# Attention softmax: the mask moves from GpSimd to VectorE, and two of eight heads are exponentiated by ScalarE straight out of PSUM

## The reference, cut to what matters

```
q, k, v = heads of layernorm(x) @ Wq + bq, ... @ Wk + bk, ... @ Wv + bv
scores  = einsum('bhqd,bhkd->bhqk', q, k) / sqrt(16)
scores  = where(adj[:, None] > 0, scores, -9e15)
attn    = softmax(scores, axis=-1)
x       = x + (einsum('bhqk,bhkd->bhqd', attn, v) as [b, n, 128]) @ Wo + bo
```

## Time and profile before

| | us |
|---|---|
| median of 3 runs | 1353.4 |
| the three runs | 1353.4, 1342.87, 1353.49 |
| the profiled execution, device time | 1348.24 |
| its span in the profile | 1346.4 |
| PE busy in the span | 1087.5 (81%) |
| DVE busy | 1032.0 (77%) |
| POOL busy | 922.8 (69%) |
| ACT busy | 837.6 (62%) |

### The profile page before, as it was taken

One profiled execution on the slowest core, in us unless ns is written; L12 is line 12 of the kernel. 1 busy time (PEld: TensorE's weight loads), 2 busy tenths in 40 slices (PEclk: granted clock), 3 DMA queues, 4 the chain that ended last, 5 costly groups with the idle time before them and its releaser, 6 DMA issues. The chain is left out here.

```text
span 1346.4 us, 39563 instructions
## 1 busy us (share of the span) xinstructions
PE 1087.5 (81%) x12580; PEld 783.5 (58%) x12581; DVE 1032.0 (77%) x2503; ACT 837.6 (62%) x1449; POOL 922.8 (69%) x929
## 2 busy tenths in 40 slices
PE   0788899889899988987288999799999999979200
PEld 0456666666666666665156677477777777768200
DVE  3578888888888888887467888487777777657498
ACT  0577777777777777774076788577766666567100
POOL 3336888888888888886766777457777777766300
PEclk9999999999999999999588999899999999999755
DMA  2113323333323333221334644244444444334399
GB/s 74 32 45 86 85 75 89 87 90 90 92 74 87 86 90 90 77 63 43 102 100 119 171 144 137 67 91 99 97 103 93 92 98 96 81 67 78 115 343 310
DMA packets 276548, 136.53 MB, mean 101 GB/s; under 512 B 195142, under 2 KB 254700, under 8 KB 276474
## 3 DMA queue, kind: packets, MB, share of 16 engines
q1 hardware_dynamic: 242938, 93.39, 28.7%
q0 software_dynamic: 16896, 33.86, 7.8%
q10 hardware_dynamic: 16640, 8.39, 2.1%
HBM read 47.95 MB, written 54.04 MB: 76 GB/s over the span
## 5 line engine op out<-in xcount | busy, mean ns | idle before, releaser
L1362 POOL DMA_INDIRECT pairs_dram<-x_rows x272 | 281.2, 1034 | 121.8 <-issue 81.8
L1040 ACT ACTIVATE hid<-Z,biases 128x512 f32<-128x512 f32 (+1 forms) x336 | 208.2, 632 | 141.1 <-PE Z L1008 88.7
L1055 DVE SCALAR_TENSOR_TENSOR h<-hid,h 128x512 f16<-128x512 f32 (+1 forms) x288 | 183.2, 649 | 54.3 <-ACT h L1031 49.6
L474 DVE TENSOR_REDUCE smax<-S 128x8 f32<-128x1024 f32 x128 | 155.8, 1217 | 73.7 <-PE S L730 72.2
L1020 PE MATMUL Y<-w,h 128*128 (+1 forms) x3168 | 192.8, 220 | 11.5 <-DVE h L1055 9.2
L1020 PEld LDWEIGHTS Y<-w,h 128*128 128x128 f16 x3168 | 185.6, 99 | 28.0 <-issue 10.6
L477 DVE TENSOR_TENSOR probs<-S,smax 128x1024 f32<-128x1024 f32 x128 | 156.8, 1225 | 14.4
L1153 POOL DMA_INDIRECT slots_dram<-x_rows,pair_slot x128 | 134.7, 1052 | 47.3 <-issue 27.3
L1008 PE MATMUL Z<-x_rows,w 128*128 128x512 f16 (+1 forms) x720 | 148.3, 352 | 11.3 <-DMA x_rows<-slots_dram 7.6
L619 ACT ACTIVATE probs<-probs 128x1024 f32<-128x1024 f32 x128 | 135.2, 1056 | 21.5 <-DVE probs L477 20.3
L339 POOL DMA_INDIRECT slots_dram<-x_rows,pair_slot x116 | 121.4, 1047 | 28.1 <-issue 16.8
(11 more groups left out here) (211 smaller groups left out, 2171.1 us busy)
## 6 DMA issues: line engine op xcount, KB each, us to landing
y_pairs<-pairs_dram SPq DMA_DIRECT2D x32, 512.0 KB, 5.9
x_res<-in_x_dram SPq DMA_DIRECT2D x32, 256.0 KB, 3.5
adj<-in_adj_dram SPq DMA_DIRECT2D x32, 256.0 KB, 3.2
xT_dram<-xT SPq DMA_DIRECT2D x32, 256.0 KB
xTu<-xT_dram SPq DMA_DIRECT2D x32, 256.0 KB, 2.9
out_dram<-x_res ACTq DMA_DIRECT2D x16, 512.0 KB, 7.9
pairs_dram<-x_rows POOLq DMA_INDIRECT x272
slots_dram<-x_rows,pair_slot POOLq DMA_INDIRECT x256
```

The costliest lines, as they stand in the source:

```text
L474: dve.tensor_reduce(smax[:].rearrange("p (r e) -> p r e", e=2), S_heads, AX_X, ALU.max).then_inc(s["max_done"], 1)
L1040: act.activation(self.hid[:, c, 0:w], self.bank(b, c)[:, 0:w], ACT.Gelu, bias=bias[:, c:c + 1], scale=1.0 / (XS * WS)).then_inc(self.gelu_ ...
L1055: dve.scalar_tensor_tensor(out=self.piece(b)[:, 1, c, 0:w], in0=self.hid[:, c, 0:w], scalar=HS, in1=self.piece(b)[:, 0, c, 0:w], op0=ALU.m ...
L1362: pool.indirect_dma_start(pairs_dram, bass.IndirectOffsetOnAxis(ap=pair_of[n][:, j:j + 1], axis=0), y_sb[n % NY][:, j], None, bounds_check ...
```

## The change

- qb, the scale of Q and the mask all change sign, so S holds minus the scores, and a masked place holds +9e15. The row maximum becomes a row minimum (smin, min_done in place of smax, max_done).
- SHIFTED = 6: VectorE subtracts for heads 0 to 5 only, as minimum minus S, with the operands swapped.
- Heads 6 and 7 (bank 3 of S) are read by ScalarE itself: one activation of 128 columns for each head, exp(-S + smin), with smin as a bias operand of one value for each partition. They stand ahead of the exponential of the other heads in ScalarE's order, and signal direct_done.
- The exponential in SBUF covers six heads.
- TensorE waits for direct_done as well as sub_done before it writes S again.
- mask moves from GpSimd to VectorE, to the end of slot 2 (mask(0) to the end of the step before group 0). GpSimd's wait for s_ps ahead of mask falls away.

```diff
+SHIFTED = 6
...
-        def mask(g, q):
-
-            pool.wait_ge(adj_loaded[q], (g // 2 + 1) * 16)
-            wait(pool, "s_ps", (g - 1) * GT)
-            pool.tensor_scalar(negmask[:, q], adj[:, q], 0.0, NEG, ALU.is_le, ALU.mult).then_inc(s["mask_ready"], 1)
...
-        mask(0, 0)
...
-            if has(g, -1):
-                mask(g + 1, (g + 1) % 2)
...
+        def mask(g, q):
+
+            dve.wait_ge(adj_loaded[q], (g // 2 + 1) * 16 if isinstance(g, int) else (g - q) * 8 + 16)
+            dve.tensor_scalar(negmask[:, q], adj[:, q], 0.0, -NEG, ALU.is_le, ALU.mult).then_inc(s["mask_ready"], 1)
...
-            dve.tensor_reduce(smax[:].rearrange("p (r e) -> p r e", e=2), S_heads, AX_X, ALU.max).then_inc(s["max_done"], 1)
-            wait(dve, "max_done", t + 1)
+            dve.tensor_reduce(smin[:].rearrange("p (r e) -> p r e", e=2), S_heads, AX_X, ALU.min).then_inc(s["min_done"], 1)
+            wait(dve, "min_done", t + 1)
             wait(dve, "pt_ps", 2 * (t - 1))
-            dve.tensor_tensor(probs[:, b].rearrange("p (r e) k -> p r e k", e=2), S_heads,
-                              smax[:].rearrange("p (r e) -> p r e", e=2).unsqueeze(3).to_broadcast([P, 4, 2, P]),
-                              ALU.subtract).then_inc(s["sub_done"], 1)
+            dve.tensor_tensor(probs[:, b, 0:SHIFTED].rearrange("p (r e) k -> p r e k", e=2),
+                              smin[:, 0:SHIFTED].rearrange("p (r e) -> p r e", e=2).unsqueeze(3).to_broadcast([P, SHIFTED // 2, 2, P]),
+                              S_heads[:, 0:SHIFTED // 2], ALU.subtract).then_inc(s["sub_done"], 1)
...
+                if j == 2 and has(g, -1):
+                    mask(g + 1, 1 - q)
...
-                act.activation(QT[:, q], M0[:, :], ACT.Identity, bias=qb[:], scale=0.25 / (XS * WS)).then_inc(s["q_sb"], 1)
+                act.activation(QT[:, q], M0[:, :], ACT.Identity, bias=qb[:], scale=-0.25 / (XS * WS)).then_inc(s["q_sb"], 1)
...
                 if has(t, 0, NT):
+                    wait(act, "min_done", t + 1)
+                    wait(act, "pt_ps", 2 * (t - 1))
+                    for h in range(SHIFTED, H):
+                        last = act.activation(probs[:, j % 2, h], S_heads[:, h // 2, h % 2], ACT.Exp,
+                                              bias=smin[:, h:h + 1], scale=-1.0)
+                    last.then_inc(s["direct_done"], 1)
                     wait(act, "sub_done", t + 1)
-                    pr = probs[:, j % 2]
+                    pr = probs[:, j % 2, 0:SHIFTED]
                     act.activation(pr, pr, ACT.Exp).then_inc(s["exp_done"], 1)
...
                     wait(pe, "sub_done", t)
+                    wait(pe, "direct_done", t)
```

More of the change, by code:

```diff
@@ L106, in attention_phase @@
     rs2s = sb("rs2s", [P, GT])
-    smax = sb("smax", [P, H])
+    smin = sb("smin", [P, H])
     turn = sb("turn_dve", [P, 1])
@@ L130, in attention_phase @@
              "top_done", "eq_done", "keyed", "key_done", "pick_done", "rest_done", "rank_ps", "counted", "slot_terms", "slot_ready",
-             "s_ps", "max_done", "sub_done", "exp_done", "pt_ps", "pt_sb", "pv_ps", "o_sb", "on_ps", "rec_done", "norm_done"]
+             "s_ps", "min_done", "sub_done", "direct_done", "exp_done", "pt_ps", "pt_sb", "pv_ps", "o_sb", "on_ps", "rec_done", "norm_done"]
     s = {n: sem(n) for n in names}
@@ L377, in _ @@
         dve.tensor_scalar(bv_mat, ones, cols[:, 2:3], None, ALU.mult).then_inc(prep, 1)
-        dve.tensor_scalar(qb[:], cols[:, 0:1], 0.25, None, ALU.mult).then_inc(prep, 1)
+        dve.tensor_scalar(qb[:], cols[:, 0:1], -0.25, None, ALU.mult).then_inc(prep, 1)
         dve.tensor_scalar(kb[:], parity[:], cols[:, 1:2], None, ALU.mult).then_inc(prep, 1)
@@ L521, in step @@
                 gather1(1, 1)
+                mask(0, 0)
                 return
@@ L673, in m0_task @@
                     wait(pe, "sub_done", NT)
+                    wait(pe, "direct_done", NT)
                 else:
```

## The result

The changed kernel takes 1387.6 us (median of 4 runs, 1386.1 to 1389.4) against 1348.1 us for the kernel before (median of 4, 1342.4 to 1353.5; the table of the time before has the median of three of them). The ratio is 1.0294, with a 95% interval from 1.0234 to 1.0353: about 39 us slower. The profiled execution has a span of 1384.8 us against 1346.4, +38.4. Of all the runs behind this text one, of the experiment "swapped", ran at a mean granted clock of 0.82 in place of about 0.94 and took 1451.9 us; it is in no median here.

What follows compares the result with a forecast made beforehand. The prediction took VectorE's chain, 18.18 us a group, as pace, replaced by a ring of 14.43 + 1.88 + 2.56 = 18.87; +0.69 over 31.75 groups is +21.9 us, 1348.2 to 1370 us. Range 1345 to 1395.

Steps and rivals of the forecast that it cites:

- a ring through ScalarE: Attention: S, PT0, pT0, PT1, pT1, direct pair, next S; 18.87 us a group against 18.18, +21.9 us; chance 0.50.
- S to pT1, four slots: Attention: from the start of the scores to the start of the second copy pT1, 14.43 us for a group.
- pT1 to the pair: ScalarE: from the start of pT1 to the start of the next activation, 0.47 us, four times 1.88 us.
- start of the pair to next S: Two direct activations of 355 ns, overlapping, 0.59 us, plus 0.05 until PE starts: 0.64, four times 2.56 us.
- 0.40 for K in slot 3: Slot 3: K's evacuation on ACT comes 0.81 us after S instead of 1.21, taking 0.40 off 14.83 us.
- the rival called dear: Attention: the direct pair with hand-over takes 0.70 to 0.80 us; at 0.76, 19.35 a group, +37 us, 1385; chance 0.16.
- its two causes: Direct pair on ScalarE: dear because the two activations don't overlap or because the waits show.
- sum of +33 us: By the skill page's activation prices, the direct pair with its hand-over is 0.73 us and the whole change +33 us.
- VectorE's gain: VectorE's subtraction shrinks from 1.23 to 0.95 us, 36 us busy over 128 tiles, but turns into idle time, worth nothing.
- more than 1 us of this idle time for each tile: Sign of being right: VectorE's idle time before the row minimum grows to over 1 us for each tile.
- "other side" rival of 1333: VectorE was the bound and is relieved; at a pair of 0.35 us, 17.71 a group, -15 us, 1333; chance 0.12.
- The mask: End of slot 2 on VectorE: 452 ns hidden in idle time, costed at nothing; 14 us without that cover.

Runs made afterwards that it cites:

- swapped: The changed kernel with TensorE's two waits ahead of the scores in the other order, direct_done first and sub_done second: 1380.6 us, ratio 1.0222 to the kernel before.
- pair_early: The changed kernel with ScalarE's direct pair moved right behind pT0, the first copy of the transposed probabilities, ahead of pT1: 1326.8 us, ratio 0.9859.
- the mask alone: The changed kernel with SHIFTED = 8: mask on VectorE and changed signs kept, no direct activations: 1350.8 us, ratio 1.0034 to the kernel before.

## Why the prediction was right, and where its size was off

**The mechanism.** The forecast was 1370 us by a ring through ScalarE, with 0.66 on slower; measured 1387.6, in the range. The ring is shown from four sides: PE waits for the direct pair in nearly every tile; two more activations lengthen three slots of four by their own length; the pair ahead of pT1 opens it and gives 61 us back; the mask changes nothing in it.

**The length, step by step,** for a group, predicted and measured in the changed kernel:

| step | predicted us | measured us |
|---|---|---|
| S to pT1, four slots | 14.43 | 3.25 + 3.49 + 3.98 + 3.64 = 14.36 |
| pT1 to the pair | 1.88 | 1.96 |
| start of the pair to next S | 2.56 | 3 x 0.76 + 0.78 = 3.06 |
| ring | 18.87 | 19.38 |

The first step, with its 0.40 for K in slot 3, held to 0.07 us. The term that was mis-sized is the third: 0.64 us for a tile, measured 0.765. Of the 0.125, 0.03 is the pair (0.62 for 0.59) and 0.09 is the hand-over to PE (0.144 for 0.05). The runs show what the 0.09 is: gone with one wait fewer, gone with the same two waits in the other order; the last section has the instruction that spends it. I had taken the hand-over from a row of a kernel in which PE waits once, and counted the added wait on PE as nothing. The miss of 0.52 for a group is 16.5 us over 31.75 groups, and the 17.6 us from 1370 to 1387.6 are this and a little of the runs' spread. So the number that came is that of the rival called dear (19.35 us for a group, 1385 us), which had a chance of 0.16. Of its two causes the first fell: the two activations do overlap (0.62 us for two of 0.369). The second, that waits show, was right in kind, but I looked for them on ScalarE between pT1 and the pair, where 0.49 us came for 0.47; they were on TensorE.

**The price of one activation.** The Trainium skill ("ScalarE: Activation LUTs", section What ACT_TABLE_LOAD costs) prices one activation of 128 columns with a pointer bias at 387 ns; the trace has 369, between that and my 355. Its sum of +33 us came nearer to the +39 than mine, but by the wrong term: it puts the pair at 0.68 us, which is 0.62, and does not have the wait on TensorE.

**VectorE's gain.** Its subtraction fell to 0.954 us as said, 35 us busy in all, and its idle time before the minimum rose from 73.7 to 120.8 us over the span. It bought nothing in the changed kernel. One sign of the prediction did not come: more than 1 us of this idle time for each tile. From 100 to 560 us it is 60.1 us for 95 tiles, 0.63 each (29.7 for 101 before), and with the mask back on GpSimd 81.1, 0.85 each: the mask fills some of it. With the ring open, the gain pays. In slot 0 of pair_early the scores start right behind the subtraction, as before, and the step from scores to scores is 3.67 us in place of 3.94, shorter by what the subtraction lost; slot 2 wins 0.50 at the median, slot 3 0.18, slot 1 nothing. That run is below both the forecast and the "other side" rival of 1333, which was priced with the old order.

**The mask.** Costed at nothing, and measured so twice within the spread of the runs: 1386.0 against 1387.6 behind the ring, 1327.3 against 1326.8 without it. The prediction allowed for a hold of up to 1.04 us by GpSimd. The rows above have it: the mask runs from 328.59 to 329.86 beside GpSimd's subtraction from 328.55 to 329.58, and is 1.27 us long. The Trainium skill ("SBUF — State Buffer", Who interferes with whom) says that tensor_scalar can enter a two-port mode, and that VectorE in such a mode and GpSimd lock each other out of a shared port pair for a whole instruction. The trace agrees in kind, with 0.418 us free and 1.27 held, to 0.28 after GpSimd's end; that the mask runs in that mode no run here shows. What was missed are the 5 us of the mask alone. The trace has 3.4 more before the last minimum, nearly all in two tiles near the start. Why the turned rows come later in the first is open; the second shows an effect that the prediction did not count: with the mask gone GpSimd runs earlier and holds other instructions of VectorE.

**The version that beats both** is pair_early at 1326.8 us, 1.4% under the kernel before (0.9% to 1.9%) and 4.4% under the changed one.

## What to carry to other kernels

Before moving work to the engine with the lowest busy share, write down what stands ahead of it in that engine's order, and who waits for its end. If the waiting one also feeds what stands ahead, the edit closes a ring, and the ring's length, not the busy share, is the new pace. The cheapest repair is then a move within the order, to a place where the engine is waiting anyway. And where an instruction waits for two things, write first the wait that is met last.

## What the runs showed of the hardware that was not expected

Two semaphore waits ahead of a matmul cost TensorE 0.09 us or nothing, by their order alone. With the wait that is met last written second, PE starts 0.15 us after ScalarE's end (pair start to scores 0.765 us); with it written first, or with only one wait, 0.06 us (0.67). In this kernel the order is worth 7 us by the medians (1387.6 against 1380.6) and 10.4 us by the last minimum of the traces.

The traces show which instruction spends the time. One tile of the changed kernel: the pair, the semaphore instruction on TensorE's weight-load queue (its start is given as 334.6), the first weight load of the scores:

```profile
333.91 0.63 ACT L620 ACTIVATE probs<-S,smin 128x128 f32<-128x128 f32 x2
...
L138 PEldq EVENT_SEMAPHORE  x1: 51/51/51, 334.6 to 334.6; - x1
...
334.66 0.34 PEld L735 LDWEIGHTS S<-KT,QT 32*128 32x128 f32 x8 [0.44 <-issue]
```

The wait that is written first (sub_done) is carried by the weight load itself; the one written second (direct_done) is an instruction of its own. In all of the middle hundred tiles that instruction starts 0.04 us after the pair's end, takes 0.051, and the weight load follows 0.025 later. In the kernel with the waits swapped the separate one is that for sub_done. In 98 of the hundred tiles it is over before the pair ends, and the weight load starts 0.05 us after the pair. With one wait there is no such instruction.
